# A decoder layer on one core: in the cross-attention chunk, the weighted sums move between the two score blocks and the projection piece to the chunk's end

## What is computed

```
q = x @ Wq.T + bq;  k = context @ Wk.T + bk;  v = context @ Wv.T + bv
# 16 heads of 16 features
scores = einsum('bhtd,bhcd->bhtc', q, k) / sqrt(16)
attn = softmax(scores, axis=-1)
out = einsum('bhtc,bhcd->bhtd', attn, v)
return out @ Wo.T + bo
```

## Time and profile before

| | |
|---|---|
| median of 3 runs | 2006.98 us (2005.32 to 2023.22) |
| the profiled execution | 2005.74 us, its span 2003.9 us |
| TensorE busy | 1838.5 us (92%) |
| VectorE busy | 1460.6 us (73%) |
| ScalarE busy | 1192.2 us (59%) |
| GpSimd busy | 438.8 us (22%) |
| mean granted TensorE clock | 0.954 |

### The profile page before, as it was taken

How to read it: one execution, slowest core, us unless ns; L and a number is a source line. 1 busy time by engine, 2 the same in 40 slices (tenths; PEclk the granted TensorE clock), 3 DMA queues, 4 the chain that set the end, 5 groups by cost and what they waited for, 6 DMA issues and landing times. The chain is left out here.

```text
span 2003.9 us, 35712 instructions
## 1 busy us (share of the span) xinstructions
PE 1838.5 (92%) x12132; PEld 951.1 (47%) x12132; DVE 1460.6 (73%) x3028; ACT 1192.2 (59%) x2430; POOL 438.8 (22%) x524
## 2 busy tenths in 40 slices
PE   6777877789999999999999999999999999789999
PEld 5655666434434444443443444444444333257875
DVE  5677675667788788778777878877887786375345
ACT  2211212047777777777777777777777777635540
POOL 2110110302211311211221131031122100026675
PEclk8989988569999999999999999999999999899999
DMA  5000002350640532253064062325307300055564
GB/s 191 1 0 0 0 0 64 93 99 2 159 92 1 120 68 65 81 106 66 16 153 84 1 120 67 67 81 106 67 10 157 55 1 2 7 189 148 167 195 128
DMA packets 67405, 151.83 MB, mean 76 GB/s; under 512 B 12384, under 2 KB 39008, under 8 KB 67104
## 3 DMA queue, kind: packets, MB, share of 16 engines
q1 hardware_dynamic: 60432, 131.20, 27.9%
q0 software_dynamic: 6816, 18.62, 3.4%
HBM read 95.82 MB, written 53.23 MB: 74 GB/s over the span
## 5 line engine op out<-in xcount | busy, mean ns | idle before, releaser
L1233 DVE TENSOR_REDUCE x_mx<-x_ps 128x1 f32<-128x512 f32 x1536 | 976.2, 685 | 218.0 <-PE x_ps L983 208.7
L1143 ACT ACTIVATE x_probs<-x_ps 128x512 f32<-128x512 f32 (+1 forms) x1664 | 894.9, 597 | 281.7 <-PE x_ps L1047 275.7
L1047 PE MATMUL x_ps<-x_qst,x_kst 50*128 50x512 f32 (+1 forms) x1664 | 595.6, 453 | 24.3 <-ACT x_probs L1143 22.1
L983 PE MATMUL x_ps<-x_kst,x_qst 48*128 48x512 f32 x1536 | 574.0, 462 | 15.4 <-DMA x_qst<-q_parts 9.0
L1031 PE MATMUL x_ps<-x_probs,x_vst 128*17 128x512 f32 (+1 forms) x3328 | 446.8, 609 | 4.8 <-ACT x_ou L1126 4.8
L983 PEld LDWEIGHTS x_ps<-x_kst,x_qst 48*128 48x128 f32 x1536 | 240.0, 191 | 433.1 <-DVE x_mx L1233 289.8
L1047 PEld LDWEIGHTS x_ps<-x_qst,x_kst 50*128 50x128 f32 (+1 forms) x1664 | 243.0, 183 | 116.7 <-ACT x_probs L1143 111.0
L1170 POOL TENSOR_TENSOR x_vst<-x_v_all,x_bv 128x768 f32<-128x768 f32 x64 | 66.6, 1067 | 387.2 <-ACT x_v_all L1101 308.5
L969 PE MATMUL x_ps<-x_ctxT,x_wk 128*128 128x256 f32 (+1 forms) x448 | 126.2, 409 | 3.9 <-PEq L65 3.9
L1763 POOL DMA_INDIRECT f_xt<-rows_x,f_ids x78 | 78.3, 1004 | 233.9 <-DVE f_ids L1940 196.0
L839 POOL TENSOR_TENSOR x_kp<-x_rest,x_zero 128x256 fp32r<-128x256 f32 (+1 forms) x105 | 59.6, 568 | 285.3 <-ACT x_rest L1121 231.3
(11 more groups left out here) (215 smaller groups left out, 2016.8 us busy)
## 6 DMA issues: line engine op xcount, KB each, us to landing
x_kst<-k_parts SPq DMA_DIRECT2D x192, 200.1 KB, 8.3
k_parts<-x_kp SPq DMA_DIRECT2D x16, 1601.0 KB, 5.7
x_ctxT<-in_ctxT SPq DMA_DIRECT2D x8, 1601.0 KB, 7.1
x_qst<-q_parts SPq DMA_DIRECT2D x192, 64.0 KB, 2.3
sorted_y<-f_yt SPq DMA_DIRECT2D x26, 384.0 KB, 3.1
q_parts<-x_qp SPq DMA_DIRECT2D x8, 1024.0 KB, 4.5
x_all<-in_x SPq DMA_DIRECT2D x8, 512.0 KB, 4.0
rows_x<-f_xn SPq DMA_DIRECT2D x8, 512.0 KB, 8.4
```

Source lines behind the costliest of these rows:

```text
L983: m = pe.matmul(o, qst[mg][rows, pair, t * P:(t + 1) * P], kst[mg][rows, pair, i * 512:(i + 1) * 512], start=True, stop=True)
L1047: pe.matmul(ps[0:w, n % S_BANKS, :], kst[g][rows, pair, c * P:c * P + w], qst[g][rows, pair, :], start=True, stop=True).then_inc(s_filled, 1)
L1143: nc.scalar.activation(probs[0:w, s % (2 * GH), :], ps[0:w, s % S_BANKS, :], ACT.Exp, scale=HD ** -0.5).then_inc(exp_done, 1)
L1233: nc.vector.tensor_reduce(out=mx[:, 2 * pair + half, t, i:i + 1], in_=o, axis=AX.X, op=ALU.max).then_inc(drained_v, 1)
```

## The change

The three parts of a chunk's plan change places: first block, second block, piece, where it was first block, piece, second block. In the loop of TensorE the weighted sums of the chunk before are issued after the first block instead of after the second, and the piece after the second. ScalarE's slices of the plan follow (first part behind the first pair, second part and piece behind the second pair). VectorE reads the parts in the new order of the list; nothing else is changed, the copy in chunk 1 neither.

```
     pieces = pieces_of(prev, following)
-    return [[(first[g][c], pieces[g][c], second[g][c]) for c in range(SC)] for g in range(G)]
+    return [[(first[g][c], second[g][c], pieces[g][c]) for c in range(SC)] for g in range(G)]
...
                     for c in range(SC):
-                        first, pieces, second = PLANS[b][g][c]
+                        first, second, pieces = PLANS[b][g][c]
                         n = woven(b, g, c, 0, n, first)
-                        for i in range(len(pieces)):
-                            fill(b, n + i, g)
-                        n = woven(b, g, c, 1, n + len(pieces), second)
                         if c:
                             values(b, g, c - 1)
                         elif b or g:
                             values(b - (g == 0), (g - 1) % G, SC - 1)
+                        n = woven(b, g, c, 1, n, second)
+                        for i in range(len(pieces)):
+                            fill(b, n + i, g)
+                        n += len(pieces)
...
-                            for item in [item for part in PLANS[b][g][c][2 * pair:2 * pair + 2] for item in part]:
+                            for item in [item for part in PLANS[b][g][c][pair:2 * pair + 1] for item in part]:
```

## The result

The change makes the kernel slower: 2098.34 us median of six runs (2090.91 to 2101.37) against 2006.15 for the kernel before (six runs beside it); the ratio is 1.044, with a 95% interval of 1.040 to 1.048. The forecast was 2088 us, between 2050 and 2119.

What follows compares the result with a forecast made beforehand. TensorE was taken to bound the cross-attention stage, any new hole being paid in full. Terms of 47.6 us on 2005.74 gave 2053.3; the clock's 33.9 made 2087.2, and the median's 1.2 more gave 2088 us, range 2050 to 2119.

Steps and rivals of the forecast that it cites:

- (1): Chunks with a piece, away from a group's start: no new wait, 3.39 us stays, cost zero.
- (2): About 65 chunks without a piece: sums wait for the last exponential, 2.71 instead of 2.63 us each, +5 us.
- (3): 21 group starts with a piece in chunk 1: sums wait for ScalarE's accumulator copy, 1.53 us each, +32.1 us.
- (4): Ten group starts without a piece: sums wait for the late copy, starting 3.20 us after block B, +13.1 us.
- (5): First batch, chunk 6: second block and sums run before the wait for the next context, -3.3 us.
- (6): Shift rows' product in chunk 10 moves 1.66 us later: bounds 0 and 4 us, taken as 0.
- (7): Granted clock at the 31 group starts with a wait: 14 falls of 3.0 us instead of three, +33.9 us.
- Rival (a): The waits come but the clock hardly falls, 0 to 3 falls: 2045 to 2054 us, chance 0.17.
- Rival (b): Nearly every group start falls in clock, 25 or more of 31: 2120 to 2138 us, chance 0.11.
- Rival (c): Bank waits and waits before the sums vanish, copy done in time: a gain, 1979 us, chance 0.04.

Runs made afterwards that it cites:

- The two halves alone: Kernel before with only the sums moved between the blocks: 2241.68 us; with only the piece moved to the chunk's end: 2129.97 us.
- the two kernels with the short filler: Old and new order, copy early, plus one 128-column float32 product in each chunk without a piece: medians 1993.36 us (old), 1998.63 us (new).
- the kernel with work in the hole: Changed kernel plus three float32 matmuls on TensorE ahead of the first sums of each group but the first: 2047.33 us median, ratio 1.018.

## Why the prediction was right, and where it was off

The direction, the place and the price of the wait were right. That the total came so near (81.5 us more forecast for the profiled execution, 85.2 measured) is in part luck: the clock cost more than forecast and the rest less.

- **(1) and (2), chunks away from the starts**: right. 13.52 instead of 13.49 us for four chunks with a piece, 2.69 us for one without in batch 7 (2.71 forecast). The ends of group 3 were mis-sized: chunks 8 to 12 became 0.7 us shorter there, where 0.08 us more was forecast for each thin one; why is open. The two halves alone show that the equality is not trivial.
- **(3), 21 starts with a piece**: right. 2.19 us from the chunk's start to the sums (2.20 forecast), stretch 7.94 instead of 6.41, so 1.53 each. With the copy moved the stretch is 6.41 again: shown, not only argued.
- **(4), ten starts without a piece**: the size is about right. The kernel after, from block B of chunk 0 on, at a start without a piece:

```profile
589.60 0.73 PE L1047 MATMUL x_ps<-x_qst,x_kst 50*128 50x512 f32 x2
...
592.77 1.91 PE L1031 MATMUL x_ps<-x_probs,x_vst 128*17 128x512 f32 x8 [1.46 <-ACT x_ou L1127]
```

The sums start 3.17 us after that block (3.20 forecast). With the clock held by the filler, chunks 1 to 4 take 13.41 us, where the kernel before takes 11.75, +1.7 (forecast 1.31, and 0.08 for each further chunk).
- **(5), the first batch**: mis-sized. Forecast -3.3 us, and the two kernels with the short filler, at a mean clock of 0.85 there in both, agree (the first group takes 53.88 us in the old order, 50.67 in the new). But the kernel after takes 49.87 us where the kernel before took 58.30: the other 5 us come mostly with the clock, at a mean of 0.80 instead of 0.73 in that group.
- **(6), the shift rows**: zero, as taken; no wait of TensorE for their landing appears.
- **(7), the clock**: right that it falls more often, wrong in how. I had 14 falls of 3.0 us each, spread evenly over the starts. There were 12: all ten starts without a piece, two of the 21 with one. And a fall costs more than before: chunks 1 to 4 take 18.6 us where the kernel with work in the hole takes 13.4, 5.2 us a fall in five of the ten. Against that kernel's stretches the 12 falls cost some 49 us, 41 more than the 8.1 of before, where I had 33.9; the medians, 2098 and 2047, say 51. So fewer falls at a higher price partly cancel. The term that was mis-sized is the share: I scaled it with the length of the wait alone, with one share for all 31 starts. With a piece before and after it, a pause of 1.5 us left the clock at 1.00 in 19 of 21 cases; behind the same pause in thin chunks the clock fell to 0.5 in ten of ten, and with the copy early, behind waits of 0.24 to 0.5 us, in six of ten. No pause of TensorE at those six starts is longer than 0.48 us in the records.

Rival (a), waits and hardly a fall, is what the kernel with work in the hole became: 2047 us, inside the 2045 to 2054 forecast for it, though 10 us of it are low clock in the last group, which the rival did not reckon with. Rival (b), 25 falls or more, is refuted by the 12. Rival (c), a gain, is refuted by the time, and by the 17.7 us of bank waits that are left and the 45.2 us of waits for the copy. What stays open is why a fall costs more in the new order than in the old, why some thin starts fall and others with the same waits do not, and why moving only the first sums makes the starts with a piece fall.

## What to carry to other kernels

When work is moved ahead in one engine's order, look at the rare step that the common case hides: here most of the 416 chunks kept their rhythm, and 31 chunks, the second of their group, waited 1.5 us for a copy whose place on the other engine was not moved along (before, ten of them waited 0.5 us). Price a pause of TensorE twice, once as its length and once as the clock it may cost, and judge the second by how thin the work around the pause is, not by the pause alone: here the same 1.5 us left the clock at 1.00 at 19 of 21 starts with a piece and lowered it at all ten without. Where a pause can't be avoided, a matmul that costs little time there can pay for itself: with the copy early, one of 128 columns per thin chunk took the median from 2025.97 to 1998.63 us in the new order and from 2004.91 to 1993.36 in the old.

## What the runs showed of the hardware

A pause of TensorE of 1.5 us left the granted clock at 1.00 in 19 of 21 cases between chunks full of matmuls (stretches of 7.93 to 7.95 us). In chunks of two blocks and sums it fell to 0.5 in ten of ten behind the same pause, and in six of ten behind waits of 0.24 to 0.5 us. At 0.5 the eight matmuls of the sums took 1.91 us (at 592.77), at 1.00 they took 1.05 (at 862.38). In the last group, where a chunk holds four scores and eight matmuls of sums only, the clock once fallen stayed at 0.5 for 41 to 61 us, in some into the stage behind it, in the profiled execution of all six experiments without the short filler (44.27 us at a mean of 0.63 with the copy early), but not in those of the kernels before and after, at 34.37 and 35.68 us and a mean of 0.90. With one float32 product of 128 columns per chunk without a piece it was 1.00 (32.34 us with the copy early). The falls go with the spread between executions of one kernel: with the copy early in the old order the mean granted clock is 0.960 in the fastest and 0.938 in the slowest of ten, 36 us apart; with the short filler it is 0.962 to 0.967, within 7 us.
